# Expert tiles taken in pairs: the order of products and turns on TensorE, the reload of shared down weights, and the place of one batch's late sums

## Chip, cores and metric

One Trainium2 chip, one NeuronCore, one launch. The metric is the device time of that core in microseconds. Three runs of the kernel before: 1117.07 us median, 1116.54 to 1117.13.

## What is computed

A decoder layer on x of shape (4, 512, 512) in fp32: causal attention with 16 heads, a selective scan in place of cross attention, two layer norms and a mixture of experts. The change lies in the experts, which come last:

```python
# 2048 tokens of width 512, 16 experts, each token goes to 2 of them
topk_indices, topk_weights = _router(x_flat, router_weight, e_bias)
# expert e:  y = relu2(x @ w_up[e]) @ w_down[e],  w_up (512, 256), w_down (256, 512)
# shared:    relu2(x @ shared_up) @ shared_down,  (512, 1024), (1024, 512)
def relu2(x):
    r = jax.nn.relu(x)
    return r * r
# out = residual + shared + sum over both choices of weight * y
```

## The kernel before

Each engine has one stream of instructions in the order in which the program writes them, and semaphores tie them together. `close()` runs the norms, the router and the shared expert; `tiles()` (from line 1895) adds the part that the change touches, for each engine one function behind the work of `close()`.

**Tiles.** The 4096 pairs of token and expert are sorted by expert into units of 64 rows, two units to a tile of 128 rows, 40 tiles in all (`SLOT_TILES`), the last ones mostly padding. The two units of a tile may belong to different experts. So each product is made in two halves of 64 rows (`halves`) that run beside each other on TensorE, the first with weights straight from `w_all`, at an address from a register that is loaded from the list of experts (`expert_of`, line 2091), the second with weights that VectorE copied to `stage_up` and `stage_down`.

**A tile's way.** GpSimd gathers 128 rows of the normed x from DRAM by an indirect DMA (`load`, line 1966, two buffers). TensorE turns them (`turn_x`, four transposes, line 1995), ScalarE copies the result out of PSUM (`copy_x`, line 2069). TensorE multiplies with the up weights (line 2022), VectorE takes relu (line 2122) and the square (line 2124), TensorE turns h (`turn_h`, two transposes, line 2003), ScalarE copies it (line 2085), TensorE multiplies with the down weights (line 2034), ScalarE copies y out (line 2082), and GpSimd scatters it to DRAM (`store`, line 1972). VectorE copies the weights of the second half: up at line 2097, down at line 2102.

**Order on TensorE.** For tile i: up products of i, down products of i-1, turn of h(i), turn of x(i+2). ScalarE: y(i-1), h(i), x(i+2). GpSimd: gather i+4, scatter i. Buffers: two of x, of its turned copy, of y and of the PSUM banks; one of h, of its turned copy and of each staged weight.

**Late sums.** The shared expert has eight chunks of 128 hidden channels. Its down products for batch 3, and chunks 2 and 3 (`PARKED`) of batch 2, are made after the tiles. Parked activations lie in DRAM meanwhile and are loaded by SyncE during the tiles (line 1945), once tile 15 is done and once tile 31 is, into room that experts no longer needed leave in `w_all`; so are two chunks of the down weights. The other six chunks (`KEPT`) of the weights stay in SBUF. After the last scatter SyncE loads the sorted y rows back (line 1956, 16 loads of 512 KB), VectorE adds both choices with their weights to the result (lines 2135 and 2137) and for batches 2 and 3 the late product from PSUM (line 2144), and SyncE writes each of the 16 pieces out (line 1960). TensorE's late products of batch 2 stand at line 2052, those of batch 3 at lines 2056 and 2058.

## Time and profile before

| | us |
|---|---|
| median of three runs | 1117.07 |
| profiled execution | 1117.31 |
| its span, first to last instruction | 1115.6 |
| PE busy | 1059.8 |
| DVE busy | 845.9 |
| ACT busy | 676.8 |
| POOL busy | 657.2 |

PE is TensorE, PEld its weight loads, DVE VectorE, ACT ScalarE, POOL GpSimd, SP SyncE. Matmuls overlap, so a busy PE need not be at its peak. Expert tiles run from about 896 to 1076 us, then the late sums and the way out. An fp32 matmul stands in the trace as two records, a transpose as one. Times in the timeline count from the first instruction.

### The profile page before, as it was taken

To read this page: it belongs to the slowest core of one execution; us is meant where nothing else is said; L and a number is where in the kernel's file an instruction comes from. 1 tells how busy PE (TensorE), PEld (TensorE's weight loads), DVE (VectorE), ACT (ScalarE), POOL (GpSimd) and SP (SyncE) were. 2 spreads that over 40 slices of the span, in tenths; PEclk is the share of its full clock that TensorE was granted. 3 is DMA by queue.
4 is the path that set the end of the run, shared out by engine and by line. 5 is a ranking of instruction groups with operands and counts; after the bars stand their busy time and mean duration, and the time that the engine had idled before them with its cause. 6 is when DMAs were issued, how large, how long until landed. Compare 5 with 4: busy or idle time off the path is not lost.

```text
span 1115.6 us, 19620 instructions
## 1 busy us (share of the span) xinstructions
PE 1059.8 (95%) x6786; PEld 620.3 (56%) x6786; DVE 845.9 (76%) x1297; ACT 676.8 (61%) x1492; POOL 657.2 (59%) x573
## 2 busy tenths in 40 slices
PE   8999988889999999999999889999999989999998
PEld 3554556666666676676666654544444445555543
DVE  6988699999999999999999989950573055555548
ACT  3876789999999999999999963512111023233210
POOL 2022299999999899999999974301115134444410
PEclk9999989999999999999999999999999999999999
DMA  7310111112111111111221008120326533443329
GB/s 226 96 39 14 28 28 35 34 40 72 34 30 39 30 40 67 39 30 37 69 86 30 29 2 281 60 76 7 126 76 217 179 116 118 135 144 120 119 105 357
DMA packets 51938, 95.05 MB, mean 85 GB/s; under 512 B 9343, under 2 KB 17535, under 8 KB 51841
## 3 DMA queue, kind: packets, MB, share of 16 engines
q1 hardware_dynamic: 45440, 74.91, 21.1%
q0 software_dynamic: 6400, 18.88, 5.3%
q8 instruction: 56, 0.92, 0.3%
q14 instruction: 42, 0.34, 0.1%
HBM read 73.72 MB, written 20.05 MB: 84 GB/s over the span
## 4 chain that ended last, share of the span: by engine, by line
PE 69%; DVE 9%; POOL 8%; ACT 8%; issue 5%; DMA 1%; SPq 0%; DVEq 0%; ACTq 0%; POOLq 0%
PE ps L1578 10%; PE ps L2022 7%; PE ps L2034 6%; PE ps L843 6%; POOL w_all L765 5%; PE ps L1592 5%; PE ps L871 4%; PE ps L832 4%; PE ps L817 4%; PE ps L358 4%; DVE w_all L1042 3%; PE ps L310 3%; ACT w_all L956 2%; PE ps L882 2%; POOL acc L773 2%
## 5 line engine op out<-in xcount | busy, mean ns | idle before, releaser
L765 POOL TENSOR_TENSOR w_all<-w_all 128x512 f32<-128x512 f32 x256 | 320.9, 1274 | 20.2 <-DVE w_all L587 14.8
L1042 DVE TENSOR_TENSOR_SCAN w_all<-ps,w_all 128x512 f32<-128x512 f32 x256 | 298.8, 1206 | 1.2 <-POOL w_all L765 0.6
L939 ACT ACTIVATE ps<-w_all,low 128x512 f32<-128x512 f32 x256 | 177.6, 697 | 1.0 <-DVE w_all L1042 0.8
L871 PE MATMUL ps<-ident,w_all 128*128 128x128 f32 x1024 | 162.1, 281 | 9.7 <-DVE acc L1050 9.5
L947 ACT ACTIVATE w_all<-ps,low 128x128 f32<-128x128 f32 (+3 forms) x256 | 132.8, 530 | 13.6 <-DVE low L1034 13.6
L871 PEld LDWEIGHTS ps<-ident,w_all 128*128 128x128 f32 x1024 | 115.0, 142 | 34.7 <-issue 20.8
L956 ACT ACTIVATE w_all<-ps 128x256 f32<-128x256 f32 (+2 forms) x192 | 101.9, 531 | 22.9 <-PE ps L832 22.6
L1034 DVE TENSOR_REDUCE low<-ps 128x2 f32<-128x256 f32 (+3 forms) x128 | 103.9, 812 | 14.5 <-PE ps L817 13.9
L1578 PE MATMUL ps<-w_all 128*128 128x512 f32 x256 | 112.1, 594 | 0.0
L832 PE MATMUL ps<-ident,w_all 128*128 128x128 f32 x640 | 108.8, 285 | 1.5 <-ACT low L1013 1.5
L843 PE MATMUL ps<-w_all,low 128*32 128x128 f32 x1280 | 95.0, 278 | 12.1 <-ACT w_all L956 10.8
L1506 POOL TENSOR_TENSOR w_all<-w_all 128x512 f32<-128x512 f32 x24 | 32.7, 1362 | 123.8 <-ACT w_all L1699 123.8
L817 PE MATMUL ps<-w_all,attn 32*128 32x384 f32 (+3 forms) x512 | 105.2, 487 | 0.0
L832 PEld LDWEIGHTS ps<-ident,w_all 128*128 128x128 f32 x640 | 70.5, 141 | 51.4 <-issue 48.2
L2082 ACT ACTIVATE attn<-ps 128x512 f32<-128x512 f32 x40 | 24.0, 600 | 120.0 <-PE ps L2034 120.0
L773 POOL TENSOR_TENSOR acc<-acc,low 128x512 f32<-128x512 f32 x64 | 81.8, 1278 | 24.8 <-ACT low L968 24.7
L1972 POOL DMA_INDIRECT sorted_y<-attn,low x40 | 40.6, 1015 | 89.7 <-ACT attn L2082 89.7
L1050 DVE SCALAR_TENSOR_TENSOR acc<-ps,low,acc 128x512 f32<-128x512 f32 x128 | 92.8, 725 | 0.0
L843 PEld LDWEIGHTS ps<-w_all,low 128*32 128x32 f32 x1280 | 60.5, 109 | 46.9 <-ACT w_all L956 24.8
L773 POOL TENSOR_TENSOR acc<-acc,w_all 128x512 f32<-128x512 f32 x64 | 81.8, 1279 | 3.6 <-ACT w_all L968 3.6
L1578 PEld LDWEIGHTS ps<-w_all 128*128 128x128 f32 x256 | 47.9, 190 | 58.4 <-issue 56.7
L2022 PE MATMUL ps<-w_all,attn 128*64 x320 | 77.6, 385 | 0.9 <-ACT attn L2069 0.6
(231 smaller groups left out, 1935.4 us busy)
## 6 DMA issues: line engine op xcount, KB each, us to landing
w_all<-b_scratch SPq DMA_DIRECT2D x64, 256.0 KB, 3.3
w_all<-sorted_y SPq DMA_DIRECT2D x18, 512.0 KB, 9.0
w_all<-in_w_up SPq DMA_DIRECT2D x16, 512.0 KB, 6.5
w_all<-in_w_down SPq DMA_DIRECT2D x16, 512.0 KB, 7.2
norms<-attn SPq DMA_DIRECT2D x4, 1024.0 KB, 4.8
out_dram<-acc SPq DMA_DIRECT2D x16, 256.0 KB, 9.9
attn<-in_x SPq DMA_DIRECT2D x3, 1024.0 KB, 6.8
attn<-in_x SPq DMA_DIRECT2D x12, 256.0 KB, 4.6
```

The source lines that it names most:

```text
L765: pool.tensor_tensor(dbu[:, k, :], keep["du"][i // N][:, k * T:(k + 1) * T], b_all[i % 2][:, :], ALU.mult).then_inc(pool_dbu.sem, pool_dbu ...
L773: pool.tensor_tensor(acc, acc, cy[n % 2][:, :], ALU.add).then_inc(pool_acc.sem, pool_acc.tick(n))
L817: last = pe.matmul(sc[:, x, 0:n], keep["attn"][r:r + DH, b, m * T + j * P:m * T + (j + 1) * P], k_4[r:r + DH, b, m // 2, 0:n], start=False ...
L832: last = pe.transpose(tb[:, at:at + P], prob[:, x, off[j] + t * P:off[j] + (t + 1) * P], ident[:, :])
L843: last = pe.matmul(ob[r:r + DH, j * P:(j + 1) * P], keep["v"][:, b * KV + m // 2, t * DH:(t + 1) * DH], prob_t[unit % 2][:, at:at + P], st ...
L871: last = pe.transpose(yb[which][:, k * P:(k + 1) * P], state[i % 2][:, k, t * P:(t + 1) * P], ident[:, :])
L939: act.activation(da[unit % 2][:, :], keep["dt"][i // N][:, k * T:(k + 1) * T], ACT.Exp, scale=keep["a_flat"][:, unit % (N * KD):unit % (N ...
L947: act.activation(prob[:, x, off[j]:off[j] + n], sc[:, x, 0:n], ACT.Exp, bias=neg_max[unit % 2][:, x:x + 1], accum_out=row_sum[unit // 8 % ...
L956: act.activation(prob_t[unit % 2][:, first * n:(first + heads) * n], tb[:, 0:heads * n], ACT.Copy).then_inc(act_turn.sem, act_turn.tick(tu ...
L1042: dve.tensor_tensor_scan(state[i % 2][:, k, :], da[unit % 2][:, :], dbu[:, k, :], 0.0, ALU.mult, ALU.add).then_inc(dve_scan.sem, dve_scan. ...
L1578: last = pe.matmul(bank[m % 2][:, :], s_up[:, k, m * P:(m + 1) * P], norm_t[b][:, k, :], start=(k == 0), stop=(k == 3))
L2022: last = pe.matmul(bank[2 + s][rows, 0:FE], x_t[s][:, k * P + n * HALF:k * P + (n + 1) * HALF], w, start=(k == 0), stop=(k == KD - 1))
```

## The change

Two tiles form a step. TensorE's order for pair g: register loads of both tiles' experts, up products of 2g and 2g+1, down products of 2g-2 and 2g-1, turns of x(2g+2) and x(2g+3), turns of h(2g) and h(2g+1). ScalarE: y(2g-2), x(2g+2), y(2g-1), x(2g+3), h(2g), h(2g+1). VectorE: both register loads, then relu, square and the up weights for two tiles later, tile by tile, then both down weights. GpSimd: two gathers, then two scatters. h, its turned copy and both staged weights get a second buffer, in room of `attn` that held down weights of the shared expert; VectorE therefore stages the first up weights only after batch 2's down products, and SyncE loads all eight chunks of the shared down weights once tile 33 is done. Both parked activations come after tile 15. The late sums of batch 2 (four adds on VectorE) are made ahead of the loop over the 16 pieces, which waits for them in batch 2. The functions `up` and `down` hold the lines of the old step with a second buffer for the staged weights and turned h.

```diff
-    stage_down = keep["attn"][:, 1, 0:FK * D]
-    stage_up = keep["attn"][:, 1, UP:2 * UP]
-    h = keep["low"][:, r["spare"]:r["spare"] + FE]
-    h_t = keep["logits"][:, :, :].rearrange("p b n -> p (b n)")
+    stage_down = [keep["attn"][:, 1 + s, 0:FK * D] for s in range(2)]
+    stage_up = [keep["attn"][:, 1 + s, UP:2 * UP] for s in range(2)]
+    h = [keep["low"][:, r["spare"]:r["spare"] + FE], keep["attn"][:, 3, 0:FE]]
+    h_t = [keep["logits"][:, :, :].rearrange("p b n -> p (b n)"), keep["attn"][:, 3, FE:2 * FE]]
...
-    rows_late = [arena[:, n * D:(n + 1) * D] for n in range(2)]
-    h_late = [[arena[:, SLOT + n * T:SLOT + (n + 1) * T] for n in range(2)], [arena[:, 2 * D + n * T:2 * D + (n + 1) * T] for n in range(2)]]
-    back = [arena[:, SLOT + 2 * T + 2 * t * D:SLOT + 2 * T + 2 * (t + 1) * D] for t in range(TT)]
+    h_late = [[arena[:, (2 * j + n) * T:(2 * j + n + 1) * T] for n in range(2)] for j in range(2)]
+    rows_late = [arena[:, 2 * SLOT + m * D:2 * SLOT + (m + 1) * D] for m in range(FS // P)]
+    back = [arena[:, 4 * SLOT + 2 * t * D:4 * SLOT + 2 * (t + 1) * D] for t in range(TT)]
...
     ONLY_0 = B * T // HALF // 2 - 1
-    ONLY_1 = 2 * B * T // HALF // 2 - 1
+    ONLY_3 = (2 * B * T // HALF + 3 - 1) // 2
 
     def run(step):
-        for i in range(SLOT_TILES + 1):
-            step(i, i % 2, (i + 2 < SLOT_TILES, i < SLOT_TILES, 0 < i))
+        for g in range(SLOT_TILES // 2 + 1):
+            pair = (2 * g, 2 * g + 1)
+            step([i + 2 for i in pair if i + 2 < SLOT_TILES], [i for i in pair if i < SLOT_TILES], [i - 2 for i in pair if i >= 2])
 
     def sync(sp):
         def load(out, in_):
-            sp.dma_start(out.rearrange("p (k c) -> p k c", k=2), in_).then_inc(s_parked, 16)
+            sp.dma_start(out.rearrange("p (k c) -> p k c", c=D), in_).then_inc(s_parked, 16)
 
         sp.wait_ge(r["s_park"].sem, r["s_park"].upto(1))
         pe_l.wait(sp, ONLY_0, "down")
-        load(arena[:, 0:2 * D], d["s_down"][PARKED[0] * P:(PARKED[-1] + 1) * P, :].rearrange("(k p) c -> p k c", p=P))
-        load(arena[:, 2 * D:2 * D + 2 * T], r["h_park"][1])
-        pe_l.wait(sp, ONLY_1, "down")
-        load(arena[:, SLOT:SLOT + 2 * T], r["h_park"][0])
+        for n in range(2):
+            load(arena[:, 2 * n * T:2 * (n + 1) * T], r["h_park"][n])
+        pe_l.wait(sp, ONLY_3, "down")
+        load(arena[:, 2 * SLOT:4 * SLOT], d["s_down"].rearrange("(k p) c -> p k c", p=P))
...
-        for i in range(SLOT_TILES):
-            if i + 4 < SLOT_TILES:
-                load(i + 4)
-            store(i)
+        for g in range(SLOT_TILES // 2):
+            for i in (2 * g, 2 * g + 1):
+                if i + 4 < SLOT_TILES:
+                    load(i + 4)
+            for i in (2 * g, 2 * g + 1):
+                store(i)
...
+        def up(i):
...
+        def down(i):
...
...
+        def step(ahead, main, lag):
+            for i in main:
...
-            if main:
+            for i in main:
+                up(i)
+            for i in lag:
+                down(i)
+            for i in ahead:
+                turn_x(i)
+            for i in main:
                 turn_h(i)
-            if ahead:
-                turn_x(i + 2)
...
-            if t == NT - 1:
-                act_l.wait(pe, LAST, "y")
-            for n in range(2):
-                last = pe.matmul(bank[4 + t][:, :], h_late[0][n][:, t * P:(t + 1) * P], rows_late[n], start=(n == 0), stop=(n == 1))
+            if t >= NT - 2:
+                act_l.wait(pe, LAST - (NT - 1 - t), "y")
+            for n, m in enumerate(PARKED):
+                last = pe.matmul(bank[4 + t][:, :], h_late[0][n][:, t * P:(t + 1) * P], rows_late[m], start=(n == 0), stop=(n == 1))
             last.then_inc(s_late_out.sem, s_late_out.tick(t))
         for t in range(NT):
             for n, m in enumerate(KEPT):
-                pe.matmul(bank[t][:, :], r["h_last"][m][:, t * P:(t + 1) * P], r["s_down_last"][m], start=(n == 0), stop=False)
-            for n in range(2):
-                last = pe.matmul(bank[t][:, :], h_late[1][n][:, t * P:(t + 1) * P], rows_late[n], start=False, stop=(n == 1))
+                pe.matmul(bank[t][:, :], r["h_last"][m][:, t * P:(t + 1) * P], rows_late[m], start=(n == 0), stop=False)
+            for n, m in enumerate(PARKED):
+                last = pe.matmul(bank[t][:, :], h_late[1][n][:, t * P:(t + 1) * P], rows_late[m], start=False, stop=(n == 1))
...
+        def copy_h(i):
+            pe_h.wait(act, i, "hT")
+            pe_l.wait(act, i - 2, "down")
+            act_h.done(act.activation(h_t[i % 2], bank[4 + i % 2][:, 0:FE], ACT.Copy), "hT")
+
+        def step(ahead, main, lag):
+            for k in range(2):
+                if lag:
+                    copy_y(lag[k])
+                if ahead:
+                    copy_x(ahead[k])
+            for i in main:
+                copy_h(i)
...
+    def stage_weights_down(dve, e, i):
+        pe_l.wait(dve, i - 2, "down")
         for n in range(2):
-            dve_d.done(dve.tensor_copy(stage_down[:, n * D:(n + 1) * D], r["w_all"][:, e, UP + n * D:UP + (n + 1) * D]), f"down{n}")
+            dve_d.done(dve.tensor_copy(stage_down[i % 2][:, n * D:(n + 1) * D], r["w_all"][:, e, UP + n * D:UP + (n + 1) * D]), f"down{n}")
...
     def first_weights(dve):
         dve.wait_ge(r["s_w_up"], 16 * E)
-        taken[0] = expert_of(dve, 1)
-        stage_first_half(dve, taken[0], 0)
+        for i in range(2):
+            taken[i] = expert_of(dve, 2 * i + 1)
+        dve.wait_ge(pe_down.sem, pe_down.upto(4 * (B - 1) - 1))
+        for i in range(2):
+            stage_weights_up(dve, taken[i], i)
 
     def vector(dve):
         dve_m.start(dve)
         pair.start(dve)
         dve.wait_ge(r["s_w_down"], 16 * E)
-        dve.wait_ge(pe_down.sem, pe_down.upto(4 * (B - 1) - 1))
...
+        def square(i):
+            pe_m.wait(dve, i, "up")
+            pe_h.wait(dve, i - 2, "hT")
+            dve_m.done(dve.tensor_scalar(h[i % 2], bank[2 + i % 2][:, 0:FE], 0.0, None, ALU.max), "relu")
+            dve_m.wait(dve, i, "relu")
+            dve_m.done(dve.tensor_tensor(h[i % 2], h[i % 2], h[i % 2], ALU.mult), "sq")
+
+        def step(ahead, main, lag):
+            for i in ahead:
+                taken[i] = expert_of(dve, 2 * i + 1)
+            for i in main:
+                square(i)
+                if i + 2 < SLOT_TILES:
+                    stage_weights_up(dve, taken[i + 2], i + 2)
+            for i in main:
+                stage_weights_down(dve, taken[i], i)
         run(step)
 
+        for t in range(NT):
+            acc = keep["acc"][:, B - 2, t * D:(t + 1) * D]
+            dve.wait_ge(s_late_out.sem, s_late_out.upto(t))
+            dve.tensor_tensor(acc, bank[NT + t][:, :], acc, ALU.add).then_inc(s_late_add.sem, s_late_add.tick(t))
...
-            n = t - (B - 2) * NT
+            if t // NT == B - 2:
+                dve.wait_ge(s_late_add.sem, s_late_add.upto(t % NT))
             pair.done(dve.scalar_tensor_tensor(acc, back[t][:, 0:D], r["weight"][0][:, t:t + 1], acc, ALU.mult, ALU.add), "first")
             pair.wait(dve, t, "first")
             second = dve.scalar_tensor_tensor(acc, back[t][:, D:2 * D], r["weight"][1][:, t:t + 1], acc, ALU.mult, ALU.add)
-            if n < 0:
+            if t // NT < B - 1:
                 pair.done(second, "second")
             else:
+                n = NT + t % NT
                 second.then_inc(s_late_add.sem, s_late_add.tick(n))
                 dve.wait_ge(s_late_out.sem, s_late_out.upto(n))
                 dve.wait_ge(s_late_add.sem, s_late_add.upto(n))
-                pair.done(dve.tensor_tensor(acc, bank[(n + NT) % (2 * NT)][:, :], acc, ALU.add), "second")
+                pair.done(dve.tensor_tensor(acc, bank[t % NT][:, :], acc, ALU.add), "second")
```

## Rows read from the trace of the kernel before

**Rows 1.** The page: the chain that ended last, shares of the span by engine
```profile
PE 69%; DVE 9%; POOL 8%; ACT 8%; issue 5%; DMA 1%; SPq 0%; DVEq 0%; ACTq 0%; POOLq 0%
```

**Rows 2.** Windows: length, busy PE, PEld, DVE, ACT, POOL, clock, DMA, GB/s
```profile
902.50:1069.52 167.02, 166.96 (x1136) 85.93 (x1136) 86.15 (x227) 52.20 (x113) 72.75 (x73) 1.00 0.37 118
...
1080.00:1115.60 35.60, 30.72 (x72) 13.33 (x70) 28.32 (x40) 0.00 (x0) 0.00 (x0) 0.96 0.91 354
```

**Rows 3.** Timeline of one tile on PE: start us, us, instruction
```profile
964.26 0.43 PE L2022 MATMUL ps<-w_all,attn 128*64 x1
...
964.53 0.38 PE L2022 MATMUL ps<-w_all,attn 128*64 x1
...
964.75 0.38 PE L2022 MATMUL ps<-w_all,attn 128*64 x1
...
967.33 0.59 PE L2034 MATMUL ps<-w_all,logits 128*64 x1
...
967.86 0.44 PE L2003 MATMUL ps<-ident,low 128*128 128x128 f32 x2
...
968.13 0.60 PE L1995 MATMUL ps<-ident,low 128*128 128x128 f32 x4
...
968.66 0.43 PE L2022 MATMUL ps<-w_all,attn 128*64 x1
```

**Rows 4.** The same timeline: ACT, POOL and DVE, idle before in brackets
```profile
963.57 0.60 ACT L2082 ACTIVATE attn<-ps 128x512 f32<-128x512 f32 x1 [3.01 <-PE ps L2034]
...
964.98 1.02 POOL L1972 DMA_INDIRECT sorted_y<-attn,low  x1 [2.10 <-ACT attn L2082]
...
966.30 0.97 POOL L1966 DMA_INDIRECT low<-norms,low  x1 [0.31 <-issue]
...
967.71 0.76 DVE L2097 COPY attn<-w_all 128x512 f32 x2 [0.57 <-issue]
...
968.77 0.60 ACT L2069 ACTIVATE attn<-ps 128x512 f32<-128x512 f32 x1
```

**Rows 5.** Line 2091 between 901 and 903 us: PE's register load of one expert
```profile
L2091 PEldq TENSOR_LOAD <-low x1: 317/317/317, 901.6 to 901.6; - x1
...
L2091 PEldq SEQ_ASSERT  x1: 26/26/26, 902.2 to 902.2; - x1
```

**Rows 6.** Timeline of the first tiles: DVE, PE and the gather at 902.54
```profile
899.63 0.42 DVE L2122 TENSOR_SCALAR low<-ps 128x256 f32<-128x256 f32 x1 [2.33 <-DMA w_all<-in_w_down]
...
901.61 0.66 PE L1995 MATMUL ps<-ident,low 128*128 128x128 f32 x4 [0.61 <-DMA low<-norms,low]
...
902.50 0.42 PE L2022 MATMUL ps<-w_all,attn 128*64 x1 [0.23 <-issue]
...
902.54 0.95 POOL L1966 DMA_INDIRECT low<-norms,low  x1 [4.22 <-PE ps L1995]
```

**Rows 7.** The first gather (line 1966), DVE beside it, a window of DMA
```profile
L1966 POOL DMA_INDIRECT low<-norms,low x1: 1064/1064/1064, 896.0 to 896.0; - x1
...
896.52 0.77 DVE L2097 COPY attn<-w_all 128x512 f32 x2 [0.50 <-issue]
...
905.50:906.00 0.50, 0.50 (x4) 0.00 (x0) 0.30 (x1) 0.00 (x0) 0.00 (x0) 1.00 0.00 0
```

**Rows 8.** Chain before the last down products, timeline of the tail, landing of stores
```profile
1074.12 0.13 issue
...
1076.12 7.13 PE L2052 MATMUL ps<-w_all 128*128 128x512 f32 x16
...
1083.20 0.75 DVE L2135 SCALAR_TENSOR_TENSOR acc<-w_all,low,acc 128x512 f32<-128x512 f32 x1 [9.10 <-DMA w_all<-sorted_y]
...
1108.84 1.88 PE L2058 MATMUL ps<-w_all 128*128 128x512 f32 x4
...
1112.29 0.69 DVE L2144 TENSOR_TENSOR acc<-ps,acc 128x512 f32<-128x512 f32 x1
...
DMA to landing us min/median/max: 2.0/9.9/14.6
```

More of the change, by code:

```diff
@@ L2002, in turn_h @@
             for f in range(FK):
-                last = pe.transpose(bank[4 + s][:, f * P:(f + 1) * P], h[:, f * P:(f + 1) * P], ident[:, :])
+                last = pe.transpose(bank[4 + s][:, f * P:(f + 1) * P], h[s][:, f * P:(f + 1) * P], ident[:, :])
             pe_h.done(last, "hT")
         turn_x(1)
-        def step(i, s, parts):
-            ahead, main, lag = parts
-            s1 = 1 - s
-            if main:
-                expert[i] = expert_of(pe, 2 * i)
-                if i == 0:
-                    pe.wait_ge(r["act_first"].sem, r["act_first"].upto(0))
-                act_x.wait(pe, i, "xT")
-                dve_m.wait(pe, i - 2, "relu")
-                for k in range(KD):
-                    if k % 2 == 0:
-                        dve_u.wait(pe, i, f"up{k // 2}")
-                    for n, rows in enumerate(halves):
-                        w = r["w_all"][:, expert[i], k * FE:(k + 1) * FE] if n == 0 else stage_up[:, k * FE:(k + 1) * FE]
-                        last = pe.matmul(bank[2 + s][rows, 0:FE], x_t[s][:, k * P + n * HALF:k * P + (n + 1) * HALF], w,
-                                         start=(k == 0), stop=(k == KD - 1))
-                pe_m.done(last, "up")
-            if lag:
-                if i == 1:
-                    pe.wait_ge(r["s_w_down"], 16 * E)
-                act_h.wait(pe, i - 1, "hT")
-                act_l.wait(pe, i - 3, "y")
-                for f in range(FK):
-                    dve_d.wait(pe, i - 1, f"down{f}")
-                    for n, rows in enumerate(halves):
-                        w = r["w_all"][:, expert[i - 1], UP + f * D:UP + (f + 1) * D] if n == 0 else stage_down[:, f * D:(f + 1) * D]
-                        last = pe.matmul(bank[6 + s1][rows, :], h_t[:, f * P + n * HALF:f * P + (n + 1) * HALF], w,
-                                         start=(f == 0), stop=(f == FK - 1))
-                pe_l.done(last, "down")
-            if main:
@@ new lines, in up @@
+        def up(i):
+            s = i % 2
+            if i == 0:
+                pe.wait_ge(r["act_first"].sem, r["act_first"].upto(0))
+            act_x.wait(pe, i, "xT")
+            dve_m.wait(pe, i - 2, "relu")
+            for k in range(KD):
+                if k % 2 == 0:
+                    dve_u.wait(pe, i, f"up{k // 2}")
+                for n, rows in enumerate(halves):
+                    w = r["w_all"][:, expert[i], k * FE:(k + 1) * FE] if n == 0 else stage_up[s][:, k * FE:(k + 1) * FE]
+                    last = pe.matmul(bank[2 + s][rows, 0:FE], x_t[s][:, k * P + n * HALF:k * P + (n + 1) * HALF], w,
+                                     start=(k == 0), stop=(k == KD - 1))
+            pe_m.done(last, "up")
@@ new lines, in down @@
+        def down(i):
+            s = i % 2
+            if i == 0:
+                pe.wait_ge(r["s_w_down"], 16 * E)
+            act_h.wait(pe, i, "hT")
+            act_l.wait(pe, i - 2, "y")
+            for f in range(FK):
+                dve_d.wait(pe, i, f"down{f}")
+                for n, rows in enumerate(halves):
+                    w = r["w_all"][:, expert[i], UP + f * D:UP + (f + 1) * D] if n == 0 else stage_down[s][:, f * D:(f + 1) * D]
+                    last = pe.matmul(bank[6 + s][rows, :], h_t[s][:, f * P + n * HALF:f * P + (n + 1) * HALF], w,
+                                     start=(f == 0), stop=(f == FK - 1))
+            pe_l.done(last, "down")
@@ L2071, in scalar, with copy_y @@
         copy_x(1)
[L2073 to L2087 removed]
+        def copy_y(i):
+            pe_l.wait(act, i, "down")
+            if i == 0:
+                act.wait_ge(r["s_park"].sem, r["s_park"].upto(1))
+            if i >= 2:
+                act.wait_ge(s_y[i % 2], i // 2 * 16)
+            act_l.done(act.activation(y[i % 2], bank[6 + i % 2][:, :], ACT.Copy), "y")
+        def copy_h(i):
[10 more added lines that the diff above has]
+                copy_h(i)
         run(step)
```

37 lines of the change are left out of this document (4 added, 33 removed).

## The prediction

> **What bounds the kernel now.** I read three views in this order: the chain that ended last, the windows, the timeline of one tile. The chain lies on PE for 69% of the span [rows 1]. In the expert tiles it is nothing else: between 902.50 and 1069.52 PE is busy for 166.96 of 167.02 us, with the clock at its upper level (1.00, 2.4 GHz) [rows 2]. That stretch holds the starts of the products of tiles 1 to 39, so 38 periods of 167.02/38 = 4.40 us. DVE (86 us), ACT (52) and POOL (73) have room in it [rows 2]. After the tiles comes a tail of 35.6 us in which DMA is 0.91 busy at 354 GB/s, DVE 28.3 us and PE 30.7 us [rows 2]: three engines near a bound, so there one engine's gain need not be the tail's.
>
> "Busy" hides small holes at the turns between kinds of work. In the timeline of one tile [rows 3] products follow each other at a fixed step: up products at 964.53 and 964.75, 0.215 apart, down products, twice as wide, 0.43 apart (estimate: twice), the last at 967.33. The turn of h starts at 967.86 instead of 967.33 + 0.43 = 967.76: 0.10 us. Its first transpose takes 0.16 instead of 0.11 (two in 0.27, four more in 0.53 - 0.10 = 0.43). After the last turn the next tile's products start 0.10 late, at 968.66, and the step after a tile's first product is 964.53 - 964.26 = 0.27 against 0.215 for the others. Together 0.10 + 0.055 + 0.10 + 0.055 = 0.31 us for one round of products, turns, products.
>
> **The change, part by part.**
>
> *Pairs on PE.* Work on PE is the same; the rounds become 20 instead of 40. A pair then takes 2 x 4.40 - 0.31 = 8.49 us if PE never waits. Laid out from the pair's start (estimates from rows 3): up products 0 to 3.50, down products to 6.93, first turn at T = 7.03, twelve transposes, next pair at T + 1.46 = 8.49. What used to hide waits is shorter or reordered, so each new wait is priced:
>
> - *x copied by ACT.* Before, x was turned a whole tile ahead. Now the turn of x(2g+2) is followed at once by its products. Turn done at T + 0.66; ACT starts 0.04 later and takes 0.60 (968.13 + 0.60, then 968.77) [rows 3, 4]; from the end of an ACT copy to the product that it releases PE needs 0.13 (after the copy of h, at 1074.12) [rows 8]. T + 1.43 against T + 1.46. Zero, with 0.03 to spare; its bound upwards is 0.2.
> - *Two register loads of the expert.* One takes PE's queue from the load's start (901.6) to the end of the check (902.2 + 0.03), 0.6 us, and the products follow 0.27 later, at 902.50 [rows 5, 6]. Two take 1.23 us. They sit behind the turns in the queue. In steady state the queue reaches them early if nothing ahead of them waits.
> - *The ring of ACT, POOL and DMA.* This is the tight one. ACT now does copy y(2g-2), x(2g+2), y(2g-1), x(2g+3). So y(2g-1), done by PE before T, is copied behind x(2g+2) and ends about T + 1.85. POOL starts the store 0.81 after the end of ACT's copy (963.57 + 0.60 to 964.98), takes 1.02, and a load comes 0.30 after that (966.30) [rows 4]. Now two loads follow, 0.97 + 0.30 each: the second starts at T + 5.25. A gather that POOL issued at 902.54, as the last turn before it ended, was the only traffic, and by 905.50 DMA was still [rows 7]: 3.0 us. Landed at T + 8.25. The turn that needs it is at T + 8.49 + 0.49. Met; but the two register loads stand behind this wait: T + 8.25 + 0.1 + 1.23 + 0.27 = T + 9.85, against the product at T + 8.49 + 1.46 = T + 9.95. Slack 0.1 us, on a sum of eight terms. Bounds: 0 to 0.45 per pair. I take 0.03, the sum's own value (none) and a little for what is not seen.
> - *DVE.* Per pair 4 x 0.43 (relu and square of two tiles), 4 x 0.76 (two copies each) [rows 4, 6] and two register loads, about 6.0 of 8.49 us. h(2g+1) is squared by 4.7, T is 7.03. Weights of the next pair's first tile are staged by 3.7. Nothing.
>
> The steady state is 18 pairs, up(2) to up(38), at 8.52: 153.4 us.
>
> *The head.* PE waits between its first and second tile: DVE waits for the last down weights until 899.63, the gather for the turn comes at 901.61 [rows 6]. In the new order up(1) runs in that hole. But DVE must load two registers (0.6 each, as the idle 0.57 before its copies [rows 4], after 899.63), relu and square tile 0, stage 0.76, relu and square tile 1: 899.63 + 1.2 + 0.1 + 0.87 + 0.85 + 0.95 = 903.6. PE's queue waits there with the turn of h(1), and only then come its own two register loads: 903.6 + 0.1 + 1.23 + 0.27 = 905.2 for up(2). Before, tile 1 started at 902.50 [rows 6] and tile 2 about a period later, near 907. The extra register loads before up(0) (0.6 us later) are covered by the same hole; without it they would cost 0.6.
>
> *The last pair.* Of its own tiles' turns only h is left. From up(38): products to 6.93, turn at 7.03, but ACT copies y(37) first, which holds it to T + 0.60 (its copies overlap by 0.1), then h(38), half as wide, 0.38, and 0.13 to PE: down(38) starts 1.12 after the turn. Then 2 x 1.72 and one 0.055 and one 0.10 for the changes of kind: 7.03 + 1.12 + 3.44 + 0.16 = 11.75 us to the first late product. In the new order: 905.2 + 153.4 + 11.75 = 1070.35.
>
> *Reloaded down weights.* SP reads all 2.1 MB in one DMA once tile 33 is done; before, half a megabyte of it. At 354 GB/s [rows 2] 5.9 us of all queues, in which POOL's last two gathers are issued. The gather of 896.00 [rows 7] reached PE at 901.61 [rows 6], after 5.6 us behind SP's weights, against 3.0 alone. Their slack is 0.1 to 1.4 us, so a single stall of 0 to 2.5 us. Tiles 34 on are mostly padding with small stores, so I take the lower part: 0.4. First late product at 1070.75; it was at 1076.12 [rows 8]. **Gain 5.4 us.** The late products then read other addresses: nothing. The two parked loads are moved together to tile 15, 1 MB as before: nothing.
>
> On that stall the Trainium skill ("DMA: Bandwidth & Descriptors", section "Queues, rings and completion order") says that each DMA engine takes turns between its queues packet by packet. By that rule a gather would be slowed by about its own moving time and the stall would be nearly zero; the row speaks rather for waiting behind what is queued.
>
> *Late sums of batch 2 first.* Four adds leave DVE's tail (the add at 1112.29 is the last of eight, 0.69 each) [rows 8], and move before 1083.20, where DVE waits 9.10 us for the first rows. Late product 3 ends at 1076.12 + 7.13 = 1083.25, so the fourth add ends 0.75 after DVE could have begun. DVE alone: 4 x 0.75 - 0.75 = 2.3 us earlier. But PE's last late product ends at 1108.84 + 1.88 = 1110.72, and the last add needs it. It starts at 1110.8 instead of 1112.29: 1.5. The last stores land 2.0 us after issue when the queue is empty [rows 8]; DMA has little left to catch up. I take **1.4 us**, bounds 0.6 to 1.6.
>
> Sum: 5.4 + 1.4 = 6.8. The profiled execution took 1117.31 us (span 1115.6), its sum is 1110.5; the median of the three runs is 0.24 lower: 1110.3.
>
> **The rivals.**
>
> *The pair waits on the ring or on register loads* (same sign, less). If the ring is longer by 0.25 than summed, 18 x (0.25 - 0.1 + 0.03) adds about 3 us: 1113.5; at the bound of 0.45, 1118. For it: two slacks under 0.1. Against: every term is a measured one.
>
> *The holes stay.* If they belong to each tile and not to the change of kind, a pair takes 8.80, 18 x 0.28 = 5.0 us more: 1115.3. Against it: between up and down products of different tiles there is none today [rows 3].
>
> *Slower: DVE's copies hold up POOL's gathers.* The first gather ran beside DVE's copy (896.52 to 897.29) and took 1.064 [rows 7], one alone 0.97 [rows 4]. Today POOL's issues fall between the copies (964.98 to 967.27, copies from 967.71) [rows 4]. In the new order the first load (T + 3.95, which is 2.5 in the next pair) runs beside the copies at 2.9 to 3.7. Price by that row 0.1, within the slack. If it waited out a pair of copies, 0.76, the ring exceeds PE by 0.66: 18 x 0.63 = 11.3 us more, 1121.6. It decides from 0.48 us of delay in the ring. The Trainium skill ("SBUF — State Buffer", section "🔬 SBUF: two separate sides") has such a rule: while DVE copies fp32 within SBUF, GpSimd cannot write DMA descriptors and is fully blocked. By the rule 1121.6; the row shows a delay of 0.1.
>
> *Better than forecast.* The stall of the reload is zero, DVE starts sooner in the head (a register load of 0.5 rather than 0.6): 1108.5.
>
> **How the numbers follow.** Forecast 0.55 (1108.7 to 1112.5, its own bounds); ring longer 0.20 (1112.5 to 1118); holes stay 0.05; slower 0.09; better 0.11 (under 1108.7). Likeliest 1110.3. Range 1107.8 to 1116.0 leaves out the slower case, the end of the ring case and a little of the better one. 0.2% (2.2 us), about what a measurement of this kernel can tell from no change, puts the border of faster at 1114.8: 0.55 + 0.11 + 0.13 + 0.03 = 0.82; same 0.08; slower 0.10.
>
> **What would show it.** Right: products of tiles 2g to 2g+2 start 8.5 us apart; PE idle under 0.1 a pair; up(2) near 905; DVE's four late adds before the first of its tail; the last add starting as PE's last product ends. Wrong: waits of PE on DMA of norms or on ACT's copy of x in every pair; POOL's indirect DMAs longer than 1.02 us beside DVE copies; a PE gap of 0.1 between up(2g) and up(2g+1). The prediction falls with any wait that repeats in each pair: 0.1 us is 1.8 us.

## The result, and the profile after

| | before | changed |
|---|---|---|
| median, first comparison (4 runs each) | 1117.1 | 1125.0 |
| median, second comparison (11 and 6 runs) | 1118.2 | 1127.1 |
| ratio to before, with 95% interval | | 1.0052 [1.0030, 1.0074] and 1.0075 [1.0061, 1.0090] |
| profiled execution, span | 1117.31, 1115.6 | 1120.17, 1118.4 |

The change makes the kernel slower, by 0.5 to 0.75%. Forecast were 1110.3 us and a range up to 1116.0. Sign and range are both wrong.

First the windows of the changed kernel's profiled execution (length; busy PE, PEld, DVE, ACT, POOL; clock, DMA, GB/s), over the 18 pairs from tile 2 on and over the tail. They answer to [rows 2].

```profile
904.44:1068.78 164.34, 154.16 (x1081) 85.04 (x1081) 83.89 (x218) 49.13 (x108) 71.11 (x71) 1.00 0.40 129
...
1080.52:1118.40 37.88, 34.60 (x82) 15.12 (x80) 28.16 (x40) 0.60 (x1) 1.73 (x2) 1.00 0.85 332
```

Before, PE was idle for 0.06 us of 167.02 in this stretch, and now it is idle for 10.2 us of 164.3. The chain on the page still lies on PE (71% now, 69% in [rows 1]) and doesn't show that.

Where the idle time lies is seen in the timeline of PE: only the first product of a pair has an idle time in brackets. Here are two turns of x and the product behind the second, in answer to [rows 3]:

```profile
911.48 1.09 PE L1998 MATMUL ps<-ident,low 128*128 128x128 f32 x8
...
919.98 1.09 PE L1998 MATMUL ps<-ident,low 128*128 128x128 f32 x8
...
922.36 0.42 PE L2022 MATMUL ps<-w_all,attn 128*64 x1 [0.85 <-ACT attn L2079]
```

The first products of the pairs stand at 904.44, 912.94, 922.36, 930.87, 940.28, 948.78, 958.31, 966.81 and so on: steps of 8.50 and of about 9.4 by turns. **8.50 us is PE's own time, forecast as 8.49; every second pair waits 0.7 to 1.1 us more.** From 1030 us on three pairs in a row wait (9.44, 8.92 and 9.31 us). Two tiles took 8.80 us before.

Between the turns at 911.48 and the product at 922.36 stand ACT and POOL (in answer to [rows 4]; idle before in brackets):

```profile
912.17 0.60 ACT L2079 ACTIVATE attn<-ps 128x512 f32<-128x512 f32 x1 [1.70 <-PE ps L1998]
912.67 0.59 ACT L2089 ACTIVATE attn<-ps 128x512 f32<-128x512 f32 x1
...
914.05 1.00 POOL L1973 DMA_INDIRECT sorted_y<-attn,low  x1 [1.73 <-ACT attn L2089]
915.36 0.99 POOL L1967 DMA_INDIRECT low<-norms,low  x1 [0.30 <-issue]
...
916.66 0.97 POOL L1967 DMA_INDIRECT low<-norms,low  x1 [0.30 <-issue]
```

Then DMA, in two windows of the same columns as above. It moves until 919.9 and not after that: the second gather takes 3.2 us from its issue, 3.0 in [rows 7].

```profile
919.50:919.90 0.40, 0.40 (x4) 0.00 (x0) 0.30 (x1) 0.00 (x0) 0.12 (x1) 1.00 0.28 113
919.90:920.20 0.30, 0.30 (x4) 0.22 (x3) 0.00 (x0) 0.00 (x0) 0.30 (x1) 1.00 0.00 0
```

Then PE's two register loads: line 2107 between 920 and 922.5 us (count, ns least/median/most, start of the first and the last), in answer to [rows 5].

```profile
L2107 PEldq TENSOR_LOAD <-low x2: 302/395/488, 920.5 to 921.2; - x2
...
L2107 PEldq SEQ_ASSERT  x2: 18/18/18, 921.1 to 921.9; - x2
```

They start at 920.5, though the turn itself ran at 919.98, and they end at 921.9. The product waits for them, not for ACT's copy of x, which the bracket names: that copy ended at 920.67 + 0.60 = 921.27.

**The reload** stands out once. SP issues all of the 2 MB at 1055.30. POOL's last two gathers stand behind it, and PE waits for both of them:

```profile
1055.30 0.37 SPq L1946 DMA_DIRECT2D w_all<-in_s_down  x1
...
1059.09 0.99 POOL L1967 DMA_INDIRECT low<-norms,low  x1 [0.30 <-issue]
1060.38 1.14 POOL L1967 DMA_INDIRECT low<-norms,low  x1 [0.31 <-issue]
...
1065.89 0.66 PE L1998 MATMUL ps<-ident,low 128*128 128x128 f32 x4 [1.32 <-DMA low<-norms,low]
...
1066.93 0.66 PE L1998 MATMUL ps<-ident,low 128*128 128x128 f32 x4 [0.38 <-DMA low<-norms,low]
```

From issue to turn the gathers take 6.8 and 6.55 us. The pair takes 1068.78 - 1057.47 = 11.31 us.

**The head and the tail.** In the head (in answer to [rows 6]) the first product of tile 0 comes 898.27 - 895.05 = 3.22 us after the start of the turn of x(1). In the trace of before the same distance is 1.27 us (895.93 to 897.20). The reason is PE's second register load, which takes 1.63 us there (third of the rows, line 2107 from 895 on). At the end (in answer to [rows 8]) DVE's last add now starts as PE's last product ends.

```profile
895.05 0.63 PE L1998 MATMUL ps<-ident,low 128*128 128x128 f32 x4 [0.20 <-ACTq L68]
898.27 0.42 PE L2022 MATMUL ps<-w_all,attn 128*64 x1 [2.60 <-DVE attn L2113]
...
L2107 PEldq TENSOR_LOAD <-low x2: 490/1062/1634, 895.1 to 895.9; - x2
...
1113.24 1.88 PE L2068 MATMUL ps<-w_all 128*128 128x512 f32 x4
...
1115.16 0.69 DVE L2172 TENSOR_TENSOR acc<-ps,acc 128x512 f32<-128x512 f32 x1 [1.20 <-PE ps L2068]
```

### The profile page after: what moved, and what is told of

Same layout as the page of the kernel before. It is cut to its first block, busy times and chain, and to the rows that moved or that the text cites. A ratio compares the mean times of both kernels' runs of the same rounds, so it can differ in the third digit from the quotient of the medians.

```text
span 1118.4 us, 19659 instructions
## 1 busy us (share of the span) xinstructions
PE 1052.7 (94%) x6786; PEld 622.2 (56%) x6786; DVE 846.8 (76%) x1297; ACT 676.4 (60%) x1492; POOL 658.5 (59%) x573
## 4 chain that ended last, share of the span: by engine, by line
PE 71%; ACT 8%; POOL 7%; DVE 6%; issue 6%; DMA 1%; DVEq 0%; ACTq 0%; SPq 0%; POOLq 0%
PE ps L1578 10%; PE ps L2022 6%; PE ps L2036 6%; PE ps L843 6%; PE ps L1592 5%; POOL w_all L765 5%; PE ps L871 4%; PE ps L358 4%; PE ps L832 4%; PE ps L817 4%; DVE w_all L1042 3%; PE ps L310 3%; ACT w_all L956 2%; PE ps L882 2%; POOL acc L773 2%
## 5 line engine op out<-in xcount | busy, mean ns | idle before, releaser
L871 PE MATMUL ps<-ident,w_all 128*128 128x128 f32 x1024 | 161.2, 280 | 10.3 <-DVE acc L1050 10.2
L2022 PE MATMUL ps<-w_all,attn 128*64 x320 | 73.3, 382 | 12.1 <-ACT attn L2079 7.8
```

Source lines behind the costliest of these rows:

```text
L871: last = pe.transpose(yb[which][:, k * P:(k + 1) * P], state[i % 2][:, k, t * P:(t + 1) * P], ident[:, :])
L2022: last = pe.matmul(bank[2 + s][rows, 0:FE], x_t[s][:, k * P + n * HALF:k * P + (n + 1) * HALF], w, start=(k == 0), stop=(k == KD - 1))
```

## The experiments

The theory with which they began: the pair waits on the ring of ACT's copies, POOL's indirect DMAs, the gather and PE's register loads (a ring is a chain of work through several engines that comes back to where it began, one round later), and once on the reload. Its rivals: DVE's copies hold up POOL; the time was lost elsewhere. Ratios are to before on the same chip, with 95% intervals. "From tile 2 on" is the time in the trace from the first up product of tile 2 to that of tile 38, 18 pairs; the changed kernel takes 164.3 us there, and 18 times 8.50 are 153.0.

**1. ACT's order.** The two copies of y first, then the two of x, so that POOL's second store starts sooner.

```
-            for k in range(2):
-                if lag:
-                    copy_y(lag[k])
-                if ahead:
-                    copy_x(ahead[k])
+            for i in lag:
+                copy_y(i)
+            for i in ahead:
+                copy_x(i)
```

> Only ScalarE's order in a pair changes: y(2g-2), y(2g-1), x(2g+2), x(2g+3) instead of y, x, y, x, so the copy of y(2g-1) ends some 1.1 us sooner and with it the scatter and the two gathers behind it. Ring theory (two pairs of tiles wait on copy of y, scatter, two gathers, turn, register loads; 17.9 us for two pairs where TensorE alone needs 17.1): two pairs fall to 17.1, so 9 rounds of 0.8 us go, about 7 us off the changed kernel, and the stall at the reload of the shared down weights shrinks by up to 1 us: 1116 to 1118. Copy theory (VectorE's copies hold up GpSimd's DMA descriptors): the gathers still run beside copies, 1123 to 1125.

Measured: 1118.41 us, ratio 0.9999 [0.9983, 1.0015]. From tile 2 on it takes 157.4 us: pairs of 8.50, but for one of 9.50, three of 8.6 to 8.7, and the pair with the reload, 11.53. At its end the clock also falls to 0.50 (1061.2 to 1064.6 us), behind a wait of 1.47 us for the gather, and the last pair takes 12.62 us to the first late product instead of 11.75. The window of the 18 pairs:

```profile
905.41:1062.83 157.42, 154.24 (x1082) 84.73 (x1082) 84.34 (x218) 50.68 (x108) 72.17 (x71) 0.99 0.42 135
```

**2. POOL's order.** One store, the two loads, the other store: the gathers no longer wait for y(2g-1).

```
-            for i in (2 * g, 2 * g + 1):
-                if i + 4 < SLOT_TILES:
-                    load(i + 4)
-            for i in (2 * g, 2 * g + 1):
-                store(i)
+            if g > 0:
+                store(2 * g - 2)
+            for i in (2 * g, 2 * g + 1):
+                if i + 4 < SLOT_TILES:
+                    load(i + 4)
+            if g > 0:
+                store(2 * g - 1)
```

> Only GpSimd's order changes: scatter 2g-2, gathers 2g+4 and 2g+5, scatter 2g-1, so the gathers no longer stand behind the scatter that comes last. Ring theory: the second gather starts about 3 us sooner after the turns, the ring falls below TensorE's 17.1 us for two pairs with 2 us to spare, and the stall at the reload falls too, since both last gathers are then issued before or as the reload starts: 1113 to 1116, and runs closer together than the 7 us of the changed kernel. Copy theory: 1123 to 1125. Theory that the reload is the main loss: 1122 or less, by what the gathers escape it.

Measured: 1117.4 us, ratio 0.9986 [0.9970, 1.0002]. From tile 2 on 155.9 us; all pairs are 8.50 but one of 8.73 and the one with the reload, 11.24.

Both edits move the gathers forward by different means, and each by itself takes nearly all of the 0.9 us out of every second pair. So the ring sets it. (In 3 of the 10 runs of experiment 1 and 5 of the 10 of experiment 2 the mean granted clock was 0.990 or lower, which bears on their medians, as told below.)

**3. The reload later.** SP waits for the last turn of x before it reads the down weights.

```
         pe_l.wait(sp, ONLY_3, "down")
+        pe_x.wait(sp, LAST, "xT")
```

> Only the start of the 2.1 MB reload of the shared down weights moves, from after the down products of tile 33 to after the turn of the last x, when no gather is left. The pair that took 11.0 us falls to 8.6 or 9.4: 2 to 2.5 us off, 1122 to 1123, with the stalls of every second pair left as they are. If the reload were the cause of the whole loss (12 us against the forecast): 1113.

Measured: 1121.55 us, ratio 1.0020 [1.0006, 1.0034]. The last pair falls from 11.31 to 9.02 us (1063.67 to 1072.69) and the others keep their waits: 162.8 us from tile 2 on. Read this late, the weights still hold up nothing: the first late product comes 11.74 us behind the start of the last pair, as in the changed kernel.

**4. The three together.**

> The three edits together: ScalarE's y, y, x, x; gathers ahead of the later scatter; reload after the last turn of x. If ring and reload are the whole cause, TensorE alone sets the pace: pairs of 8.57 us, 18 of them 154.3 us from tile 2's up products at 904.4, then 11.75 to the first late product, at 1070.5 instead of 1080.5 in the profiled run, so 1110 us and a spread of runs below 2 us. If something else bounds the pairs (VectorE's copies, register loads on TensorE's queue by themselves), 1115 or more and pairs over 8.8 us.

Measured: 1110.95 us, ratio 0.9941 [0.9921, 0.9961], faster than both kernels. From tile 2 on:

```profile
905.77:1059.10 153.33, 153.08 (x1082) 84.01 (x1082) 86.94 (x218) 49.73 (x106) 69.41 (x71) 1.00 0.38 125
```

PE is idle for 0.25 us of 153.3, the forecast's steady state (153.4). What the forecast said of PE was right; its ring and its reload were not. One pair of the 18 takes 8.78 us: it starts at 973.80, just behind SP's issue of the two parked loads (1 MB, from 972.52 on). The pair in that place is the longer one in experiments 1, 2, 8, 10 and 11 too (8.73 to 9.50 us), though not in experiment 6 (8.50); the prediction had put those loads at nothing, and no run moved them.

**5. The late sums alone.** The kernel before, with batch 2's four late adds ahead of the loop.

```
+        for t in range(NT):
+            acc = keep["acc"][:, B - 2, t * D:(t + 1) * D]
+            dve.wait_ge(s_late_out.sem, s_late_out.upto(t))
+            dve.tensor_tensor(acc, bank[NT + t][:, :], acc, ALU.add).then_inc(s_late_add.sem, s_late_add.tick(t))
         for t in range(TT):
```

> The kernel before with one part of the change alone: batch 2's four late sums go ahead of DVE's tail. My theory of the tail (it then ends with PE's last late product, as the changed kernel's trace shows): 1.4 to 1.6 us faster than before, and the last add of DVE starts as PE's last product ends. Rival: the tail's gain comes from its DMAs or from the other addresses of the late products, then this kernel is within 0.5 us of before.

Measured: 1118.12 us, ratio 0.9989 [0.9977, 1.0000], some 1.3 us less than before, with an interval that just reaches no change. The trace is clearer. From the first late product to the end of the span it takes 38.03 us, where before took 39.46, and DVE's last add starts 0.04 us after PE's last product has ended at 1115.50:

```profile
1113.62 1.88 PE L2058 MATMUL ps<-w_all 128*128 128x512 f32 x4
...
1115.54 0.69 DVE L2150 TENSOR_TENSOR acc<-ps,acc 128x512 f32<-128x512 f32 x1 [1.20 <-PE ps L2058]
```

The tail is as forecast.

**6. PE's register loads ahead of the turns.** They leave the ring and nothing else changes.

```
-            for i in main:
-                expert[i] = expert_of(pe, 2 * i)
             for i in main:
                 up(i)
             for i in lag:
                 down(i)
+            for i in ahead:
+                expert[i] = expert_of(pe, 2 * i)
             for i in ahead:
                 turn_x(i)
```

> The changed kernel with PE's two register loads of a pair moved ahead of the turns of x, so that they no longer stand behind the gather in PE's queue. Theory of the ring (gather landed, release, 2 register loads 1.2 to 1.5 us, products): the ring loses at least 1.2 us per two pairs, more than the 0.8 to 0.9 that it is too long, so pairs are 8.50 us apart except the one with the reload, and the time falls by about 7 us, to 1117 to 1118. Rival, the gathers themselves are late by more than the ring (POOL held up, or DMA latency): the next pair still waits for most of the 0.9, the time falls by under 3 us.

Measured: 1114.1 us, ratio 0.9960 [0.9946, 0.9974]: 10 to 13 us below the changed kernel by the ratios, more than the 7 expected. In two pairs PE has no idle time now:

```profile
914.80:931.81 17.01, 17.01 (x121) 9.29 (x120) 9.36 (x24) 5.47 (x13) 8.23 (x8) 1.00 0.37 117
```

From tile 2 on it takes 156.5 us, 7.9 less than the changed kernel, so the theory's 7 are met there. The first pair is 5.06 us instead of 6.17, because two register loads went out of it as well, which I had not counted. The remaining 1 to 4 us are not in the pairs; the granted clock below bears on them.

**7. DVE's copies of up weights twice.** Four more copies in each pair, into an unused place.

```
         for n in range(2):
+            if i + n > 0:
+                dve_u.wait(dve, i + n - 1, f"x{1 - n}")
+            dve_u.done(dve.tensor_copy(keep["attn"][:, 3, D:2 * D], r["w_all"][:, e, n * D:(n + 1) * D]), f"x{n}")
             dve_u.done(dve.tensor_copy(stage_up[i % 2][:, n * D:(n + 1) * D], r["w_all"][:, e, n * D:(n + 1) * D]), f"up{n}")
```

> The changed kernel with each of DVE's copies of up weights done twice (one into an unused place), so 4 more copies of 0.38 us in each pair. Theory of the ring, with no lock between DVE's copies and POOL's descriptors: the indirect DMAs keep their 0.97 to 1.15 us and the 2.4 us from a store to its landing; DVE has room for 1.5 us, so the time moves by less than 2 us. Rival, DVE's copies hold up POOL: twice as many copies beside the gathers, so twice the delay, indirect DMAs of 1.3 us or more, and 5 to 10 us more in all.

Measured: 1121.32 us, ratio 1.0040 [1.0021, 1.0059], not slower than the changed kernel. POOL's indirect DMAs in 15 pairs of this kernel, then of the changed one (count, busy us, mean ns, idle before):

```profile
L1973 POOL DMA_INDIRECT sorted_y<-attn,low x30 | 32.7, 1089 | 61.0 <-ACT attn L2089 61.0
L1967 POOL DMA_INDIRECT low<-norms,low x30 | 31.3, 1045 | 9.1 <-issue 9.1
```

```profile
L1973 POOL DMA_INDIRECT sorted_y<-attn,low x30 | 30.4, 1015 | 65.1 <-ACT attn L2089 65.1
L1967 POOL DMA_INDIRECT low<-norms,low x30 | 30.1, 1004 | 9.1 <-issue 9.1
```

60 more copies of 0.42 us, and POOL's 60 instructions are longer by 0.07 and 0.04 us. From tile 2 on the trace takes 163.4 us, against 164.3. In the same stretch 15 of the stores have 1.4 us of copies beside them on average and take 1.17 us, and the other 15 have none and take 1.00. So an effect is there, but about an eighth of the time of the copies, and the rival "DVE's copies hold up POOL's gathers" falls: its price was 0.76 us a pair. The rule behind it is in the Trainium skill ("SBUF — State Buffer", section "🔬 SBUF: two separate sides"): while DVE makes an fp32 copy within SBUF, GpSimd is locked out and can't write DMA descriptors. A full lock is not what these rows show.

**8. The three, with the late sums back in the loop.** The edit of experiment 5 undone on experiment 4.

> The changed kernel with ACT's order, POOL's order and the later reload (the three edits together gave 1110.95 us), but with batch 2's late sums back in the loop of the tail. If the part for the late sums is worth in this kernel what it is worth by itself: 1.4 to 1.6 us slower than the three edits together, 1112.4 to 1112.6 us. Rival, worth nothing once the tail starts earlier (DMA ends it): same as 1110.95 within 0.5.

Measured: 1114.93 us, ratio 0.9961 [0.9946, 0.9975], 0.0020 (2.2 us) above experiment 4, though the two intervals overlap, and more than the 1.4 to 1.6 us expected. The trace agrees: 40.13 us from the first late product to the end, against 37.94 in experiment 4, 2.2 us. The add that now stands last waits for nothing but DVE's turn, 2.25 us after PE's end at 1109.98:

```profile
1112.23 0.69 DVE L2168 TENSOR_TENSOR acc<-ps,acc 128x512 f32<-128x512 f32 x1
```

**9. The changed kernel again.**

> The changed kernel itself once more, beside the kernel before, since its median rests on 4 runs. Its expert tiles and its tail together are 1.7 us longer than before's in the traces (from the first up product of tile 0 to the end of the span 220.15 us against 218.4). If that is all, the median is 1 to 3 us above before's; if the 8 us of the first comparison are typical, there are longer waits in the tiles in most executions than in the one that was profiled, and a second profile should show some of them: pairs over 9.6 us.

Measured: 1127.1 us, ratio 1.0075 [1.0061, 1.0090]. The second of the two cases, but not in the place that was expected: two pairs are over 9.6 us (9.89 and 10.10, besides the one with the reload), but from tile 2 on the second trace takes 163.6 us (164.3 in the first). Its extra 6 us lie ahead of tile 2, whose products start at 910.71 instead of 904.44. 3.3 us have come about before the expert tiles: the last transpose ahead of them ends at 898.1 instead of 894.8, most of it (2.9) in the stretch between 663 and 690 us, which the change doesn't touch. PE has no work there for 3.02 us in both traces, and in this one its clock is at 0.50 behind that (first row), in the first trace at 1.00. The other 3.0 us are the first pair, 9.16 us instead of 6.17, with PE at its lower clock (0.50, 1.2 GHz) after an idle time of 2.6 us (898.95 to 901.55; second row):

```profile
665.30:672.10 6.80, 5.88 (x13) 3.45 (x14) 2.20 (x4) 2.56 (x5) 1.33 (x1) 0.50 0.00 1
...
901.55:907.00 5.45, 5.45 (x26) 3.21 (x28) 1.52 (x4) 0.00 (x0) 0.00 (x0) 0.50 0.44 175
```

**10. The reload in halves.** POOL's order of experiment 2; 1 MB where 2 MB started, 1 MB after the last turn.

```
-        load(arena[:, 2 * SLOT:4 * SLOT], d["s_down"].rearrange("(k p) c -> p k c", p=P))
+        load(arena[:, 2 * SLOT:3 * SLOT], d["s_down"][0:4 * P, :].rearrange("(k p) c -> p k c", p=P))
+        pe_x.wait(sp, LAST, "xT")
+        load(arena[:, 3 * SLOT:4 * SLOT], d["s_down"][4 * P:8 * P, :].rearrange("(k p) c -> p k c", p=P))
```

> The changed kernel with POOL's order (alone it left all pairs at 8.50 but the one with the reload, 11.24), and the reload of the down weights cut in two: 1 MB where the 2 MB started, 1 MB after the last turn of x. Theory, the last gathers wait behind what SP has queued, in proportion to it: half of it costs them at most 3 us instead of 4, of which POOL's order leaves over 0.8 of slack, so that pair takes 8.5 to 10.0 us and the kernel is 1.2 to 2.7 us faster than with POOL's order alone. Rival, the wait does not go by the amount that is queued (the gathers wait for the place of the transfer, or for something else at that point): the pair stays at 11 us.

Measured: 1111.11 us, ratio 0.9937 [0.9924, 0.9950]. The pair takes 8.50 us, at the lower end of the forecast, where experiment 2 has 11.24 with these two waits (rows of experiment 2):

```profile
1059.89 0.66 PE L2000 MATMUL ps<-ident,low 128*128 128x128 f32 x4 [0.90 <-DMA low<-norms,low]
1061.37 0.66 PE L2000 MATMUL ps<-ident,low 128*128 128x128 f32 x4 [0.82 <-DMA low<-norms,low]
```

So the wait goes by how much is queued at that place. The whole gain over experiment 2 (0.0049, 5.5 us) is more than these 2.7; in the pair lists nothing else has changed by more than 0.2 us, but none of the 5 runs here had a mean clock of 0.990 or less.

**11. The three, and the register loads early.**

> The three edits (ACT's order, POOL's order, the later reload) and PE's register loads ahead of the turns of x, all together. Since the three edits already bring all pairs but one to 8.50 us, PE's own time, more slack in the ring has nothing left to remove: 1110 to 1111.5 us when before is at 1117 to 1118, a ratio of 0.993 to 0.995. Rival, slack is still worth something in executions in which DMA is late: up to 1 us faster than the three edits, and a narrower spread.

Measured: 1110.97 us, ratio 0.9935 [0.9921, 0.9949]. No difference from experiments 4 and 10 that these runs can tell: with PE idle for next to nothing, more slack has nothing to remove. (The pair behind the parked loads took 9.36 us all the same.)

**12. One register load at a time in the head.** The changed kernel, tile 1's loads on PE and on DVE moved behind tile 0's work.

```
             for i in main:
-                expert[i] = expert_of(pe, 2 * i)
+                if i > 1:
+                    expert[i] = expert_of(pe, 2 * i)
             for i in main:
+                if i < 2:
+                    expert[i] = expert_of(pe, 2 * i)
                 up(i)
```

> The changed kernel, but in the first pair each register is loaded only ahead of its own tile (on PE and on DVE), so that tile 0's products start after one load. In the traces of the changed kernel PE's second load there takes 1.64 us instead of 0.30 and the first product comes 3.22 us after the last turn of x, against 1.27 before; in the second of them the granted clock then falls to 0.50 for about 6 us, and the first pair takes 9.16 us. Theory A, this idle time costs only through the clock (otherwise the wait for the last down weights covers it): the first product about 1.3 us after the turn, the clock stays at its upper level in the head in most executions, and the median is 1 to 3 us below the changed kernel's: a ratio of 1.0045 to 1.0065 against its 1.0052 and 1.0075, with the pairs from tile 2 on as they were (8.50 and about 9.4). Theory B, the head's lateness has nothing to do with it: the same median as the changed kernel within 1 us, 1.0065 to 1.0085.

Measured: 1123.82 us, ratio 1.0042 [1.0028, 1.0057]. The ratio lies just under theory A's 1.0045, but the edit didn't do what it was meant to. The first product still comes 3.05 us after the start of the turn, now held up by DVE, whose own second load has become the long one:

```profile
902.26 0.68 PE L2022 MATMUL ps<-w_all,attn 128*64 x1 [2.42 <-DVE attn L2116]
...
L2110 DVEq TENSOR_LOAD <-low x2: 546/950/1354, 898.8 to 900.0; - x2
```

The granted clock fell to 0.50 here too. So this run does not decide between A and B.

## Why the prediction was wrong

By its own steps, on the profiled execution (forecast 1110.5, measured 1120.17):

| step | forecast | trace | difference |
|---|---|---|---|
| head, up(2) starts | 905.2 | 904.44 | -0.8 |
| 18 pairs on PE alone | 153.4 | 153.0 | -0.4 |
| waits in the pairs | in the above | 8.5 | +8.5 |
| stall of the reload | 0.4 | 2.8 | +2.4 |
| last pair | 11.75 | 11.74 | 0 |
| first late product to the end | 38.06 | 37.92 | -0.1 |

Together +9.6 (9.7 before rounding). The step that failed is **the ring of ACT, POOL and DMA**, "Slack 0.1 us, on a sum of eight terms". Counted from T = 911.48:

| term | forecast | trace |
|---|---|---|
| second gather issued | T + 5.25 | T + 5.18 |
| landed | T + 8.25 | T + 8.4 |
| queue free for the register loads | 0.1 | 0.6 |
| two register loads | 1.23 | 1.4 |
| to the product | 0.27 | 0.46 |
| product | T + 9.85 | T + 10.88 |

The chain was right and so were ACT's and POOL's terms. Four small terms behind the issue were each too short, by 1.1 us in all (1.0 with the issue, which came 0.07 us sooner), against a slack of 0.1. The largest is the queue: its loads start 0.6 us after the gather has landed, and between the two stand the eight transposes in PE's queue. I had put 0.1 there with no row for it. Next come the register loads, 0.30 us for the first and 0.49 for the second; I had read it in one place [rows 5]. A sum whose slack is a hundredth of its length is not "zero and a little"; its likeliest value was some tenths late, at 1.8 us for each tenth in every pair.

The forecast also took the ring as a price per pair. The trace pays it in every second pair, so 0.47 on average, just beyond the bound of 0.45. The reason is where the ring begins and ends: it begins at the turn of x, which was on time at 919.98, and ends at the product behind it, which was late at 922.36. The next turn comes 9.42 us later (929.40) instead of 8.50, so the next round has 0.9 us more and nothing waits. The rival **"the pair waits on the ring or on register loads"** was the true one. It had 0.20 and a price that ended at 1118, since the reload's stall was priced apart from it. In its sum, 18 x (0.25 - 0.1 + 0.03), the 0.03 should be taken off, as in the sum of the slower rival: 2.2 us more and not 3.

**The reload.** The bounds were 0 to 2.5 us and it was 2.8. I took "the lower part" for the small stores of tiles that are mostly padding. But the stall comes from gathers behind 2 MB, and experiment 10 shows that half of it at that place costs nothing. On that place the text weighed the Trainium skill ("DMA: Bandwidth & Descriptors", section "Queues, rings and completion order"), by whose turns between queues the stall was nearly zero. The trace disagrees: 6.8 and 6.55 us from issue to turn, where 3.2 is usual from issue to landing. The text had said which of the two the row spoke for, and the sum then went nearly by the other.

**The head.** up(2) was right, for this execution. "The extra register loads before up(0) (0.6 us later)" were not: the second load took 1.63 us, and tile 0's product came 1.95 us later after the turn than before. The hole covered it in time, but PE is idle meanwhile.

**From the profiled execution to the median.** The forecast moved by -0.24 us here. In the two comparisons the changed kernel's medians lie 5 to 7 us above its first profiled execution, and before's less than 1 above its own. Each run lists its mean granted clock. It is 0.990 or lower in 24 of 90 runs of the kernels with pairs (in 6 of 10 of the changed kernel itself, at 1125 to 1128 us), in 2 of 12 of experiment 5, and in none of 79 of before. In runs at 0.997 the changed kernel took 1120.17 us (one run) and before 1116.1 to 1118.4 (14 runs): there they differ by the 3 us of the two traces. At 0.992 and 0.991 they differ by more: 1124.96 and 1127.57 us (one run each), against medians of 1119.4 (19 runs) and 1121.1 (3 runs) before.

The traces show two places where the lower clock (0.50) costs PE time. One is the stretch behind the 3.02 us without work at 663 us, which no edit touches: nine of the fourteen traces have the lower clock there, experiment 5's among them, and lose 1.3 to 2.9 us. The other is the head. In the traces of experiments 3, 8, 9, 10 and 12, behind 2.4 to 2.6 us without work, the first pair takes 7.5 to 9.2 us, with 6.17 in the changed kernel's first trace; the other seven traces with pairs, with 2.4 to 3.0 us of idle time there, keep the upper level. Nor is before's order free of it. In experiment 5, behind 1.39 and 0.62 us without work, tile 1 takes 5.73 us instead of 4.40, with this row in it:

```profile
905.40:908.80 3.40, 3.40 (x18) 1.94 (x18) 0.40 (x2) 0.60 (x1) 0.95 (x1) 0.50 0.19 39
```

So nearly all of the 6 us between the two traces of the changed kernel (2.9 and 3.0) stand at the lower clock in these two places. That the change makes it more frequent, and that this explains the further 4 to 5 us of the medians, is argued from the counts of runs and not shown, as experiment 12 failed to remove the idle time. Why the changed kernel's runs have the low mean more often than those of experiments 4, 6 and 10, with nearly the same head (1 of 6, 0 of 8, 0 of 5 runs), stays open.

**Right:** no hole between products of one kind, 0.31 us less for two tiles (8.50 against 8.80); ACT's copy of x hidden where the ring is not late; DVE's work within the pair; the last pair; the tail, which PE ends, by 1.4 us in experiment 5 alone too (2.2 in experiment 8); DVE's copies no obstacle to POOL. The time of the whole idea with two reordered queues and one wait more, 1110.95 us, is near the forecast's number, and its ratio to before (0.9941, 6.6 us) near the forecast's gain of 6.8.

## What to carry to other kernels

Grouping work to save changes of kind on the bounding engine also doubles what stands in a row on the engines around it; write out the longest ring through all queues, the instructions of the queue itself included, and where its slack is below a few tenths of a microsecond, change the order (stores that release nothing behind loads, register loads ahead of a wait) instead of trusting the sum. A large transfer that nobody needs yet belongs behind the last small one that somebody waits for. And read several executions: where one profile shows a hole that costs nothing, the next may show the lower clock behind it.

## What was not expected of the hardware

- A register load took 0.30 us in most places, but as PE's second in the head 1.61 to 1.65 us in ten of the eleven traces that have it there, and 1.41 in the other. It began while POOL was writing the first gather's descriptors and in the ten ended 0.01 to 0.07 us after POOL's second instruction (here 896.41 + 1.12 = 897.53, the load at 897.57). In experiment 12 DVE's second load took 1.35 in the same place, and ended 0.3 before POOL's. That POOL's descriptors hold these loads up fits most of the ends, but was not tested.
- Gathers behind a 2 MB transfer took 6.5 to 8.5 us from issue to turn, where PE waited for them; behind 1 MB so little that the pair kept its 8.50 us.
- The start of the expert tiles differs by up to 4.5 us between the traces, up to 3 of it from one stretch (663 to 690 us) that no edit touches and in which the clock is at either of its levels. Two traces have to be compared from a common point behind it.
